# VectorE's norm, spectrum and weight-mixing steps cut at each dependent link, with the merge strings written anew

## What is computed

```
for two layers:                                   # conditional convolution
    rw  = sigmoid(mean_hw(x) @ Wr + br)           # router, 4 experts
    Wk  = sum_e rw_e * Wpw_e ; h = relu(bn(x @ Wk + rw @ bpw))      # 24 -> 96
    h   = relu(bn(sum_e rw_e * (depthwise3x3_e(h) + bdw_e)))
    x   = bn(h @ sum_e rw_e * Wpwl_e + rw @ bpwl) + x               # 96 -> 24
t = tokens(x)
t = t + attention(ln(t))      # linear attention, ln: (t - mean) / sqrt(var + eps)
t = t + ffn(ln(t))            # 24 -> 96 -> 24, operands rounded to fp8 (5 bit exponent)
t = t + fourier(ln(t))        # 1x1, 2-d FFT, complex mix with relu, inverse FFT, 1x1
t = t + ffn(ln(t))
```

## Time and profile before

| | |
|---|---|
| three timed runs, median | 2370.8 us (2369.45 to 2375.8) |
| the profiled execution | 2371.59 us, of which the span of its core is 2369.8 us |
| granted TensorE clock, mean | 0.917 |
| busy: PE, VectorE, ScalarE, GpSimd | 2066.6, 1931.3, 1583.3, 116.1 us |
| instructions of VectorE in the profile | 3745 |

### The profile page before, as it was taken

One profiled execution on the slowest core, in us unless ns is written; L12 is line 12 of the kernel. 1 busy time (PEld: TensorE's weight loads), 2 busy tenths in 40 slices (PEclk: granted clock), 3 DMA queues, 4 the chain that ended last, 5 costly groups with the idle time before them and its releaser, 6 DMA issues.

```text
span 2369.8 us, 48881 instructions
## 1 busy us (share of the span) xinstructions
PE 2066.6 (87%) x19720; PEld 1219.0 (51%) x19720; DVE 1931.3 (81%) x3745; ACT 1583.3 (67%) x2704; POOL 116.1 (5%) x290
## 2 busy tenths in 40 slices
PE   5687988998889999999889997999899997987765
PEld 2233434663447635664447634475366734763653
DVE  5986989799969898899869997898989997475353
ACT  4345457766777687766867676776877677657644
POOL 0001000001000010000000000000000000000000
PEclk9987989999999899999979998999999998885865
DMA  5001001000020002000020002000010000000000
GB/s 151 1 1 21 1 1 22 2 2 1 4 39 2 2 1 41 3 2 1 4 39 2 2 1 42 1 2 2 1 33 2 2 1 21 2 2 1 22 1 21
DMA packets 108592, 29.63 MB, mean 13 GB/s; under 512 B 104144, under 2 KB 104272, under 8 KB 107984
## 3 DMA queue, kind: packets, MB, share of 16 engines
q1 hardware_dynamic: 108368, 26.50, 5.5%
HBM read 16.85 MB, written 9.63 MB: 11 GB/s over the span
## 4 chain that ended last, share of the span: by engine, by line
DVE 47%; PE 32%; ACT 12%; issue 7%; SPq 1%; DMA 1%; ACTq 0%; DVEq 0%; POOL 0%; POOLq 0%
DVE acc L1522 23%; PE P L771 5%; PE P L750 5%; PE P L986 4%; DVE SQ L1687 3%; DVE arena L1671 3%; PE P L999 2%; PE P L1078 2%; DVE T L1701 2%; PE P L923 2%; DVE T L1538 2%; DVE arena L1687 2%; PE P L820 2%; DVE roots L1687 2%; PE P L810 1%
## 5 line engine op out<-in xcount | busy, mean ns | idle before, releaser
L1522 DVE SCALAR_TENSOR_TENSOR acc<-H,Dm,acc 128x784 f32<-128x784 f32 x1024 | 997.4, 1030 | 41.5 <-ACT acc L1155 41.1
L750 PE MATMUL P<-T,Wk 112*128 112x448 f32 (+1 forms) x768 | 386.5, 593 | 52.5 <-ACT H L1148 29.0
L771 PE MATMUL P<-H,diag 64*64 64x392 f32 x4608 | 409.8, 496 | 14.0 <-DVE T L1538 12.6
L1148 ACT ACTIVATE H<-P,biasA 128x448 f32<-128x448 f32 (+1 forms) x384 | 237.5, 621 | 179.1 <-PE P L750 161.8
L771 PEld LDWEIGHTS P<-H,diag 64*64 64x64 f32 x4608 | 166.7, 133 | 223.7 <-issue 190.0
L750 PEld LDWEIGHTS P<-T,Wk 112*128 112x128 f32 x768 | 132.0, 201 | 167.8 <-ACT H L1148 90.0
L1178 ACT ACTIVATE acc<-P,biasT 128x392 f32<-128x392 f32 x128 | 71.8, 587 | 93.7 <-PE P L771 93.5
L1155 ACT ACTIVATE acc<-H,Dm 128x784 f32<-128x784 f32 x128 | 121.5, 949 | 11.9 <-PE P L793 9.9
L1184 ACT ACTIVATE acc<-acc,biasA 128x784 f32<-128x784 f32 x128 | 119.3, 946 | 6.6 <-DVE acc L1522 6.4
L1011 PE MATMUL P<-pack_b,arena 128*96 128x112 f32 x928 | 111.5, 268 | 13.3 <-DVE arena L1687 6.9
L793 PE MATMUL P<-acc,Wk 128*64 128x392 f32 (+1 forms) x512 | 104.9, 533 | 18.4 <-ACT acc L1184 18.3
(11 more groups left out here) (210 smaller groups left out, 3594.2 us busy)
## 6 DMA issues: line engine op xcount, KB each, us to landing
xin<-in_x SPq DMA_DIRECT2D x224, 42.0 KB, 2.2
out_y<-arena SPq DMA_DIRECT2D x8, 1176.0 KB, 6.0
pack_b<-in_pack_b SPq DMA_DIRECT2D x1, 3870.5 KB, 15.6
arena<-in_pack_s SPq DMA_DIRECT2D x1, 1584.0 KB, 6.8
pack_a<-in_pack_a SPq DMA_DIRECT2D x1, 1084.0 KB, 5.5
pack_i<-in_pack_i SPq DMA_DIRECT2D x1, 320.0 KB, 3.1
arena<-in_pack_k SPq DMA_DIRECT2D x1, 192.0 KB, 3.3
```

What stands on the lines that cost most here:

```text
L750: pe.matmul(conv_rows(slice(0, 128), HB[(NP * s + e) % len(HB)], n), Wk1[:, 128 * j:128 * (j + 1)], image_rows(T[q % TB], a, n), start=Tru ...
L771: last = pe.matmul(conv_rows(slice(64 * h, 64 * (h + 1)), CVB + r, HH), diag[64 * r:64 * (r + 1), tap, :], H1[64 * r:64 * (r + 1), slot(s, ...
L1148: act.activation(H1[:, slot(s, j), o:o + n, 1:1 + HW], conv_rows(slice(0, 128), HB[(NP * s + e) % len(HB)], n), ACT.Relu, bias=biasA[:, j, ...
L1522: ins = ve.scalar_tensor_tensor(a, H1[:, slot(s, j), r:r + SR, c:c + HW], Dm[:, j, tap:tap + 1], a, ALU.mult, ALU.add)
```

## The change

Three places in the code of VectorE get `yield`s at their links, and the wait goes behind the `yield`, so that `TURNS` can put another stream's step into the gap: one in each of three links of the mixing, five per layer norm, one per group of the spectrum. No instruction is added or taken away on any engine. All four strings are new, since they count steps; those of PE, ScalarE and GpSimd count the same steps in another order.

```diff
 # TURNS, the first line of "vector" (all of the four strings are replaced)
-        "c27 d2 c17 d1 c2 d1 c14 d1 c4 d1 c3 m1 d2 c23 d2 c15 d1 c1 d1 c16 d1 c2 d1 c10 d2 m1 c1 m1 c1 m2 c1 "
+        "c25 d1 c4 d1 c16 d2 c15 d1 c1 d1 c9 d2 c6 m1 c19 d1 c2 d1 c15 d1 c2 d1 c14 d1 c1 d1 c11 d2 c2 m2 c4 "
 # router, the mixing (the link of Wks and the first of biasA in the same way)
-                link(ve.tensor_tensor(mixk[:, :, :], par[f"wkx{L}"][0:R, :, :],
-                                      rw[0:R, 0:E].unsqueeze(1).broadcast_to([R, HID + 1, E]), ALU.mult), q, "conv")
+                done = link(ve.tensor_tensor(mixk[:, :, :], par[f"wkx{L}"][0:R, :, :],
+                                             rw[0:R, 0:E].unsqueeze(1).broadcast_to([R, HID + 1, E]), ALU.mult), q, "conv", wait=False)
+                yield
+                ve.wait_ge(chain_c.sem, done)
 # layer_norm
                 yield
                 ve.wait_ge(norm.sd_ready.sem, norm.sd_ready.at(q, i + 1))
-                link(ve.reciprocal(norm.rstd, norm.sdev), q, half)
-
+                done = link(ve.reciprocal(norm.rstd, norm.sdev), q, half, wait=False)
+                yield
+                ve.wait_ge(chain.sem, done)
                 rest, (high, middle_, low) = norm.sdev, norm.terms
                 ve.tensor_copy(high, norm.rstd).then_inc(norm.term_ready[0].sem, 1)
+                yield
                 ve.wait_ge(norm.term_ready[0].sem, norm.term_ready[0].at(q, i + 1))
-                link(ve.tensor_tensor(rest, norm.rstd, high, ALU.subtract), q, half)
+                done = link(ve.tensor_tensor(rest, norm.rstd, high, ALU.subtract), q, half, wait=False)
+                yield
+                ve.wait_ge(chain.sem, done)
 ...
 # fourier
                         if dst is m13_g and k == 1:
-                            link(last, q, "back")
+                            read = link(last, q, "back", wait=False)
+                            yield
+                            ve.wait_ge(chain_b.sem, read)
```

More of the change, by code:

```diff
@@ L1486, in router @@
                                  rw[:, E:16].rearrange("p (j e) -> p j e", j=NT).unsqueeze(2).broadcast_to([128, NT, DCOL, E]), ALU.mult)
-                link(ve.tensor_tensor(mixk[:, :, :], par[f"wkx{L}"][0:R, :, :],
-                                      rw[0:R, 0:E].unsqueeze(1).broadcast_to([R, HID + 1, E]), ALU.mult), q, "conv")
+                done = link(ve.tensor_tensor(mixk[:, :, :], par[f"wkx{L}"][0:R, :, :],
+                                             rw[0:R, 0:E].unsqueeze(1).broadcast_to([R, HID + 1, E]), ALU.mult), q, "conv", wait=False)
+                yield
+                ve.wait_ge(chain_c.sem, done)
                 ve.tensor_reduce(Dm[:, :, :].rearrange("p j t -> p (j t)"), mixd[:, :, :, :].rearrange("p j t e -> p (j t) e"), AX.X, ALU.add)
-                link(ve.tensor_reduce(Wks[:, :], mixk[:, :, :], AX.X, ALU.add), q, "conv")
+                done = link(ve.tensor_reduce(Wks[:, :], mixk[:, :, :], AX.X, ALU.add), q, "conv", wait=False)
+                yield
+                ve.wait_ge(chain_c.sem, done)
                 ve.tensor_tensor(Wk1[:, :].rearrange("p (i m) -> p i m", i=QI), Wks[:, 0:HID].unsqueeze(1).broadcast_to([R, QI, HID]),
@@ L1496, in router @@
                 ve.tensor_scalar(bias3[:, :], Wks[:, HID:HID + 1], bn3s[L][:, 0:1], bn3s[L][:, 1:2], ALU.mult, ALU.add)
-                link(ve.tensor_tensor(biasA[:, :, :], Dm[:, :, NTAP:NTAP + 2], bns[L][:, :, :], ALU.mult), q, "conv")
+                done = link(ve.tensor_tensor(biasA[:, :, :], Dm[:, :, NTAP:NTAP + 2], bns[L][:, :, :], ALU.mult), q, "conv", wait=False)
+                yield
+                ve.wait_ge(chain_c.sem, done)
                 link(ve.tensor_tensor(biasA[:, :, :], biasA[:, :, :], bnc[L][:, :, :], ALU.add), q, "conv")
@@ L1544, in layer_norm @@
                 NSP = len(spread)
+                chain = {"middle": chain_m, "back": chain_b}[half]
                 yield
                 ve.wait_ge(norm.sd_ready.sem, norm.sd_ready.at(q, i + 1))
-                link(ve.reciprocal(norm.rstd, norm.sdev), q, half)
+                done = link(ve.reciprocal(norm.rstd, norm.sdev), q, half, wait=False)
+                yield
+                ve.wait_ge(chain.sem, done)
                 rest, (high, middle_, low) = norm.sdev, norm.terms
                 ve.tensor_copy(high, norm.rstd).then_inc(norm.term_ready[0].sem, 1)
+                yield
                 ve.wait_ge(norm.term_ready[0].sem, norm.term_ready[0].at(q, i + 1))
-                link(ve.tensor_tensor(rest, norm.rstd, high, ALU.subtract), q, half)
+                done = link(ve.tensor_tensor(rest, norm.rstd, high, ALU.subtract), q, half, wait=False)
+                yield
+                ve.wait_ge(chain.sem, done)
                 ve.tensor_copy(middle_, rest).then_inc(norm.term_ready[1].sem, 1)
+                yield
                 ve.wait_ge(norm.term_ready[1].sem, norm.term_ready[1].at(q, i + 1))
-                link(ve.tensor_tensor(low, rest, middle_, ALU.subtract), q, half)
+                done = link(ve.tensor_tensor(low, rest, middle_, ALU.subtract), q, half, wait=False)
+                yield
+                ve.wait_ge(chain.sem, done)
                 for k, t in ((1, 1), (1, 2), (1, 3), (2, 0), (2, 1), (2, 2), (2, 3)):
```

## The result

Four runs of the changed kernel have a median of 2340.19 us (2335.14 to 2343.58), four of the kernel before in the same study 2371.3 us. The ratio is 0.9868, with a 95% interval of 0.9852 to 0.9884. A second measurement, beside the last experiments, gave 2340.54 us. The direction was forecast; the size was not: 31 us instead of 12. The median lies 0.2 us inside the lower end of the stated range (2340 us), which is luck: that end stood for rival (c), not for the sum.

The account below looks back on a forecast made before the run. The prediction saw a body with PE (92%) and VectorE (89%) both nearly full, and a thin tail of dependent chains. Gains of 5 + 1 + 1.5 + 4 = 11.5 us gave 2359 us, 8-in-10 range 2340 to 2382 us.

Parts of the forecast that it names:

- rival (c): Whole body: new strings also take a tenth of VectorE's 200 us open time, 20 us more, 2339 us in full; chance 0.12.
- part 4: End of last convolution: five taps move into idle time among ffn 0's steps of quad 6; 4 us gained.
- Part 1: VectorE's links: 73 divided at 0.12 us each take 8.8 us off VectorE; 5 us of the run gained.
- Part 2: Start of quad 0's second layer: sixth addition and first tap come earlier, `setup_rest` in front of the tap; 1 us gained.
- Part 3: Start of quad 1: router ahead of quad 0's norm 0 shortens the way from mixing to first tap; 1.5 us gained.
- rival (a): Nothing seen: PE paces the body, ffn 0's steps wait for ScalarE and PE; 2368 us, chance 0.25.
- Rival (b): Slower: taps in links lengthen norms, each quad-to-quad distance grows 3 us; 2380 us, chance 0.21 with other worse-string effects.

Follow-up runs that it names:

- e13: Changed kernel with all 73 divided links closed, each group standing where its last part stood: 2361.62 us.
- e5: Changed kernel, same order, but at the touched links VectorE waits at once, before the other stream's step: 2347.21 us.
- e7: Changed kernel with GpSimd's fills of ones row and padding held behind VectorE's shifts, in all quads: 2350.4 us.
- e17: The changed kernel run once more, unaltered, as base for experiments on it: 2340.54 us.
- e10: Changed kernel with `setup_rest` back in front of the last two additions of quad 0's first layer: 2346.58 us.
- e16: Changed order on all four engines until the middle of quad 1's convolution, order of the kernel before from there: 2364.97 us.
- e3: Order of the kernel before until quad 7's convolution begins, changed order from there: 2373.62 us.
- e2: Kernel before, its order kept, but in 29 norm links the next tap moves up into the link: 2385.48 us.
- e4: Order of the kernel before until quad 4's convolution begins, changed order from there: 2358.06 us.
- e6: Kernel before with GpSimd's fills (ones row in quads 1, 2, 5, and padding) held behind VectorE's shifts: 2362.68 us.

## Why the prediction fell short, point by point

The step that failed is what the prediction put at nothing: the new order of the streams in the body, and with it all that dividing a group does beyond the overlap. The sum priced a divided link at its 0.12 us alone, gave the new strings only the named places of parts 2 to 4, and left the rest to rival (c) with a chance of 0.12. The runs show 14 us for groups that can be interrupted (e13 against e5) and 10 us for the new order with every link closed (e13 against before). What it did price came to 13 us where 11.5 were forecast (7 for the overlap, 6.4 for the start, which is a part of the 10, and nothing for part 4). That this is close is luck: the errors of parts 3 and 4 have opposite signs.

- **Direction, tail, VectorE as one of two full engines: right.** The tail kept its 354 us. The mark moved by 32.6 us and the time by 31.
- **Part 1, the links: the price was right, the part was incomplete.** 0.12 us per link was forecast and 0.13 measured; 5 us of the run were forecast and 7 measured (e5). But dividing a link does one more thing, which no term had. It lets VectorE serve another stream in the middle of a group that lasts 3.6 us: closing the 73 links costs 21 us at the better of two places (e13), 14 more than losing the overlap alone. Beside that the shifts took 8.5 us less. Little of it comes from the divisions, since with all links closed they take 44.3 to 45.2 us, against 43.5 and 52.0; most is the new order of GpSimd and VectorE against each other, which the prediction had put at 0.
- **Part 2, quad 0's second layer: at the tap the clock hides it, at the end it is more than forecast.** In the first trace of the changed kernel the sixth addition came earlier, but by 3.9 us and not 5.7, and PE's diagonal matmuls took 8.98 us instead of 7.50:

```profile
95.96 0.61 DVE L1547 SCALAR_TENSOR_TENSOR T<-P,bias,T 112x392 f32<-112x392 f32 x1
...
109.42 0.63 DVE L1547 SCALAR_TENSOR_TENSOR T<-P,bias,T 112x392 f32<-112x392 f32 x1 [4.32 <-PE P L796]
...
132.46 1.98 DVE L1531 SCALAR_TENSOR_TENSOR acc<-H,Dm,acc 128x784 f32<-128x784 f32 x2
```

```profile
96.64 8.98 PE L774 MATMUL P<-H,diag 64*64 64x392 f32 x72 [1.99 <-DVE T L1547]
...
108.49 1.53 PE L796 MATMUL P<-acc,Wk 128*64 128x392 f32 x8 [0.80 <-ACT acc L1187]
```

  The last additions stand at 109.42 us instead of the forecast 106.8, and the first tap at 132.46 instead of 128.7. The clock has a part in that. From 94 to 109 us (a stretch, columns as in the earlier trace rows) the granted clock was 0.72 in the changed kernel, and 0.89 in e7, whose order is the same up to there and whose diagonal matmuls took 7.85 us:

```profile
94.00:109.00 15.00, 11.02 (x86) 3.95 (x86) 11.10 (x15) 2.74 (x4) 0.15 (x1) 0.72 0.00 0
```

```profile
94.00:109.00 15.00, 10.26 (x88) 3.90 (x88) 11.76 (x20) 2.74 (x4) 0.15 (x1) 0.89 0.00 0
```

  The first tap of e7 came at 129.0 us, and that of e17, the changed kernel again, at 128.4 us, with its last additions at 106.2 and the granted clock at 0.89: there the forecast held. Thirteen traces have the changed order up to this tap; it comes between 127.8 and 132.8 us, on average at 130.5. Six have that of before, with 128.6 to 131.8 us, on average 130.3. So the single trace above does not show a loss, and the forecast gain of 1.3 us at the tap is too small to be seen. Putting the setup back cost 6 us at the end (e10), against 1 us forecast for this part.
- **Part 3, quad 1's start: the term was mis-sized.** Forecast 1.5 us, at most 3; the stretch from the 65th to the 129th tap is 10 us shorter, and it is so in all: 85.6 to 87.7 us in the thirteen traces, 94.7 to 96.2 in the six. 8 of the 10 us are gaps. I had bounded it by the time from the mixing's first instruction to the tap. What moved stands ahead of that: the router is no longer behind norm 0 of quad 0.

```profile
205.03 0.17 DVE L1482 TENSOR_TENSOR rw<-P,pack_a 128x16 f32<-128x16 f32 x1 [1.15 <-PE P L739]
205.78 0.85 DVE L1557 RECIPROCAL mid<-mid 128x112 f32<-128x112 f32 x1 [0.57 <-ACT mid L1212]
...
207.30 0.60 DVE L1488 TENSOR_TENSOR acc<-pack_a,rw 128x420 f32<-128x420 f32 x1 [0.42 <-ACT rw L1140]
...
218.70 1.03 DVE L1531 SCALAR_TENSOR_TENSOR acc<-H,Dm,acc 128x784 f32<-128x784 f32 x1
```

  The mixing (L1488) starts at 207.30 us instead of 213.80, because `rw` (L1482) stands in front of the reciprocal and not behind the norm. From the mixing to the first tap it is 11.4 us, before 12.46; that 1.1 us is all that the term had looked at. The bound was taken from the wrong start. To the end, parts 2 and 3 are worth 6.4 us (e16).
- **Part 4, the end of the last convolution: wrong.** Forecast 4 us, measured none (e3). The reciprocal came 13 us closer behind the last tap, where 4 were forecast, and the idle time between the two went from 12 to 3 us, but ffn 0's steps wait for ScalarE and PE, and putting taps between them made the taps later and not the steps sooner. This is what rival (a) had said of it.
- **Rival (b), slower norms: its mechanism is real and its condition decides.** In the old order 29 divided links cost 14 us (e2), with PE waiting for the shifts. In the new order it does not appear, since PE's waits for `thirdsm` stay small: 5.8 us idle in the group before L838, where the earlier trace rows have 12.1. Its idle time in the group for `thirdsb` rose from 12.1 to 16.6 us.
- **Rival (c), more from the new order as such: this is what came.** It had a chance of 0.12. The condition for being wrong was written down: a body that moves by more than 10 us, since only the links were priced in it. It did: quad 1's first tap was 7.6 us ahead, norm 2 of quad 6 32.6 us, and 13.6 us come from quad 4 on (e4), where the prediction had nothing but links and part 4.

**What stays open.** Of the 31 us, 7 are the overlap and 14 the interruptible groups (e5, e13), measured in the new order and each known to some 6 or 7 us; 10 are that order without any division. Which places of the order make those 10, beyond the start (6.4 us) and the collisions (8 us in the old order, not additive here), isn't settled. Swapping VectorE's string alone, or those of the other engines alone, wasn't tried, so how much of the 10 us one engine's order alone would bring is open.

## What to carry to other kernels

A string of short dependent instructions is best priced three times: the gap between two of them (0.12 us here), what it holds up while it can't be interrupted (up to 14 us for 73 links here, twice the overlap), and what it collides with. Dividing it is no gain by itself: 29 divisions in the old order cost 14 us, because PE stood waiting for the end of the chain. Idle time in front of a step says nothing about whether the step can come sooner; look at who ends that wait. And before a us or two at one instruction is explained, a second trace of the same kernel shows how far it moves by itself.

## What the hardware showed that was not expected

- A bf16 copy of 0.18 us on VectorE stood for 2.69 us beside a 2.7 us fill on GpSimd, and holding that fill back was worth 8 us of 2371 (e6).
- A tap between two dependent instructions of VectorE is overlapped on both sides, by 0.07 and 0.08 us in the norm shown; with the waits ahead of it VectorE takes 0.13 us more for each of the 73 links (e5).
- The same instructions of PE, 72 matmuls with little around them, took 6.16 us in e13, 7.76 in e17, 7.85 in e7 and 8.98 in the changed kernel, whose orders are the same up to there; the granted clock of the 15 us around them was 1.00, 0.89, 0.89 and 0.72. The tap that follows came between 127.8 and 132.8 us in thirteen traces of that order.
